# A four-layer conditioned residual block on one core: x1 as one fp32r product over 96 stacked rows, the class product over all 128 rows, and new stage orders before and after the loop

## The reference

```python
# layer 0: a low-rank product with weights of each entry's own (rank 30)
U = (mu @ W_dec + b_dec).reshape(B, 257, 30); param = einsum('bik,kj->bij', U, V)
x = x + (einsum('bsd,bde->bse', x, param[:, :-1]) + param[:, -1][:, None])
# layer 1: modulated linear layer
x = x + clip(einsum('blc,oc->blo', x * styles[:, None], weight) * dcoefs[:, None] + bias, -256, 256)
# layer 2: down to 64, relu, up to 256, both with weights scaled per entry
x = x + (relu(x @ w_down) @ w_up + x)
# layer 3: layer norms with gains picked by pathway, class and time ids, concatenated, MLP, layer norm
h = ln(ln(x, pw_g[pathway], pw_b[pathway]), cp_g[comp], cp_b[comp]); t = ln(x, tm_g[time], tm_b[time])
s = ln(x, ms_g[scale], ms_b[scale]);  m, n, r = x + mlp_ln(memory / noise / resource state)
x = x + ln(silu(cat([w0*h, w1*t, w2*m, w3*n, w4*r, w5*s]) @ W1 + b1) @ W2 + b2)
```

## Time and profile before

| | before |
|---|---|
| median of 3 runs | 523.67 us (523.2 to 524.6) |
| the profiled execution | 521.21 us, of which the span is 519.4 us |
| mean granted TensorE clock | 0.994 of full speed |
| busy: PE, PE weight loads | 486.3 us (94%), 354.2 us (68%) |
| busy: DVE, ACT, POOL | 405.8 us, 336.3 us, 391.0 us |
| DMA | 61.78 MB, mean 119 GB/s |

### The profile page before, as it was taken

One profiled execution on the slowest core, in us unless ns is written; L12 is line 12 of the kernel. 1 busy time (PEld: TensorE's weight loads), 2 busy tenths in 40 slices (PEclk: granted clock), 3 DMA queues, 4 the chain that ended last, 5 costly groups with the idle time before them and its releaser, 6 DMA issues.

```text
span 519.4 us, 9425 instructions
## 1 busy us (share of the span) xinstructions
PE 486.3 (94%) x3198; PEld 354.2 (68%) x3198; DVE 405.8 (78%) x696; ACT 336.3 (65%) x638; POOL 391.0 (75%) x367
## 2 busy tenths in 40 slices
...
GB/s 299 247 304 208 203 20 124 163 73 135 83 127 81 77 171 56 191 24 223 0 229 17 205 43 173 74 136 112 106 142 63 175 47 90 49 21 145 40 2 81
DMA packets 34989, 61.78 MB, mean 119 GB/s; under 512 B 5017, under 2 KB 17413, under 8 KB 34580
## 3 DMA queue, kind: packets, MB, share of 16 engines
...
q10 hardware_dynamic: 864, 0.61, 0.4%
...
## 4 chain that ended last, share of the span: by engine, by line
PE 79%; POOL 6%; DVE 5%; DMA 4%; issue 3%; ACT 2%; SPq 0%; DVEq 0%; POOLq 0%; ACTq 0%
PE ps_c L902 11%; PE ps_c L904 11%; PE ps_c L903 10%; PE ps_d L948 9%; PE ps_d L962 5%; PE ps_a L976 5%; PE ps_b L902 3%; PE ps_b L903 3%; PE ps_b L904 3%; PE ps_b L935 2%; PE ps_a L988 2%; DMA set_wdec<-in_nets_rows 2%; PE ps_a L994 2%; PE ps_b L994 2%; DMA set_wdec<-in_W_dec 1%
## 5 line engine op out<-in xcount | busy, mean ns | idle before, releaser
L1507 POOL DMA_INDIRECT pw_rows<-in_pw,gidx x64 | 65.0, 1016 | 17.9 <-issue 17.4
L948 PE MATMUL ps_d<-xm_t,l_w 128*128 128x512 f32 x128 | 59.0, 603 | 2.2 <-POOL xm_t L1516 2.2
L1209 ACT ACTIVATE h<-h,nb_h,rstd_h 128x256 f32<-128x256 f32 x64 | 33.3, 591 | 33.1 <-POOL nb_h L1531 33.0
L1240 ACT ACTIVATE tm_t_h<-ps_a 128x1024 fp32r<-128x1024 f32 x16 | 16.4, 1026 | 45.6 <-DVE ps_a L1413 45.6
L1516 POOL TENSOR_TENSOR xm_t<-x_t,style 128x1024 f32<-128x1024 f32 x16 | 30.5, 1905 | 20.2 <-DVE x_t L1345 20.1
L948 PEld LDWEIGHTS ps_d<-xm_t,l_w 128*128 128x128 f32 x128 | 23.1, 190 | 26.8 <-issue 24.2
L1546 POOL TENSOR_TENSOR h<-xhat,pw_rows 128x1024 f32<-128x1024 f32 x16 | 38.0, 2378 | 4.1 <-ACT xhat L1209 4.1
L1565 POOL TENSOR_TENSOR w_up<-up_rep,ugub 128x1024 f32<-128x1024 f32 x16 | 38.0, 2372 | 2.2 <-issue 2.0
L1551 POOL TENSOR_TENSOR h<-h,pw_rows 128x1024 f32<-128x1024 f32 x16 | 38.3, 2394 | 1.3
L1567 POOL TENSOR_TENSOR w_up<-w_up,ugub 128x1024 f32<-128x1024 f32 x16 | 38.1, 2382 | 1.3
L902 PE MATMUL ps_b<-w_h,act_t_l 128*128 128x256 f32 x128 | 37.7, 294 | 0.4 <-DVE act_t_l L1450 0.4
...
## 6 DMA issues: line engine op xcount, KB each, us to landing
...
pw_rows<-in_pw,gidx POOLq DMA_INDIRECT x64, 3.7
...
```

The lines of the kernel that those rows point to most:

```text
L948: m = eng.matmul(ps_l1[:, o, :], l1_w[:, k, o * P:(o + 1) * P], xm_t[:, k, :], start=k == 0, stop=k == KB - 1)
L1209: m = eng.activation(out[:, j, :], src[:, j, :], ACT.Identity, bias=nb[k][:, j:j + 1], scale=rstd[k][:, j:j + 1])
L1507: eng.indirect_dma_start(pw_rows[c.ring][:, j, :], None, t["pw"], bass.IndirectOffsetOnAxis(ap=gidx[c.ring][:, j:j + 1], axis=0)).then_inc ...
```

## The change

Six edits, the last one in all engines but SP:

1. V is loaded over 96 rows (three copies). `act_vhigh` makes its fp32r copy `v_st`, `v_vlow` replaces rows 64 to 95 by V's low half. `t_st` becomes 96 rows of fp32r.
2. `act_th1` copies t to a tile of its own (`t_f`, in the free rows of the index tile), `act_th2` writes three rounded copies of it instead of one, and a new stage `g_tlow` on POOL replaces the first by t's low half.
3. `pe_x1` makes, per half of the features, one fp32r matmul over the 96 rows.
4. `pe_cp` multiplies over all 128 rows where it took strips of 24, and `v_gains` leaves the second strip's class columns at zero.
5. `v_pads` clears all of `gain_tab` and `t_st` as well.
6. New `begin` and `end` tables on PE, ACT, DVE and POOL; in the loop's tables only `(g_tlow, 2)` is new.

```diff
         def pe_x1(eng, c):
...
-            wait(eng, a_th, c.n + 1)
+            if first(c):
+                eng.wait_ge(c_v, 2)
+            wait(eng, a_th, 2 * c.n + 2)
+            wait(eng, g_tl, c.n + 1)
             for k in range(KB):
-                rows = slice(k * RP, k * RP + RK)
-                m = eng.matmul(ps_x1[:, k, :], v_rep[rows, k * P:(k + 1) * P], t_st[rows, :], start=True, stop=True)
+                m = eng.matmul(ps_x1[:, k, :], v_st[:, k * P:(k + 1) * P], t_st[:, :], start=True, stop=True)
...
         def pe_cp(eng, c):
-            for j in (0, 2, 1, 3):
-                rows = slice(j // 2 * STRIP, j // 2 * STRIP + CLS)
-                m = eng.matmul(out[:, j, :], onehot[c.ring][rows, j * P:(j + 1) * P], gain_tab[rows, 0:D],
-                               start=True, stop=True)
+            for j in range(CT):
+                m = eng.matmul(out[:, j, :], onehot[c.ring][:, j * P:(j + 1) * P], gain_tab[:, 0:D], start=True, stop=True)
...
         def act_th1(eng, c):
-            wait(eng, p_x1, c.n)
-            out = t_st[0:RK, :].rearrange("r (q j s) -> r q j s", j=4, s=S)
+            wait(eng, g_tl, c.n)
+            out = t_f.rearrange("r (q j s) -> r q j s", j=4, s=S)
...
         def act_th2(eng, c):
-            wait(eng, a_th1, c.n + 1)
-            eng.activation(t_st[RP:RP + RK, :], t_st[0:RK, :], ACT.Copy).then_inc(a_th, 1)
+            wait(eng, a_th, 2 * c.n + 1)
+            wait(eng, p_x1, c.n)
+            for lo in (0, RP, 2 * RP):
+                m = eng.activation(t_st[lo:lo + RK, :], t_f, ACT.Copy)
+            m.then_inc(a_th, 1)
...
+        def act_vhigh(eng, c):
+            eng.wait_ge(d_wts, 48)
+            eng.activation(v_st[:, :], v_rep[:, :], ACT.Copy).then_inc(c_v, 1)
+        def v_vlow(eng, c):
+            eng.wait_ge(c_v, 1)
+            low = slice(2 * RP, 3 * RP)
+            eng.tensor_tensor(v_st[low, :], v_rep[low, :], v_st[low, :].bitcast(F32), ALU.subtract).then_inc(c_v, 1)
+        def g_tlow(eng, c):
+            wait(eng, a_th, 2 * c.n + 2)
+            low = t_st[0:RK, :]
+            eng.tensor_tensor(low, t_f, low.bitcast(F32), ALU.subtract).then_inc(g_tl, 1)
...
-                             (pe_dec, 11), (pe_style, 0), (pe_dec, 12), (pe_dec, 13), (pe_dec, 14), (pe_dec, 15),
+                             (pe_dec, 5), (pe_style, 0), (pe_dec, 6), (pe_dec, 7), (pe_dec, 8), (pe_dec, 9),
```

More of the change, by code:

```diff
@@ L188, in conditioned_residuals @@
         ugub = sb("ugub", [P, CT, 2 * D])
-        idx_ch = [sb(f"idx_ch{r}", [CLS, CH], I32) for r in range(2)]
+        idx_t = [sb(f"idx_t{r}", [2 * RP, CH]) for r in range(2)]
+        idx_ch = [tile[RP:RP + CLS, :].bitcast(I32) for tile in idx_t]
+        t_f = idx_t[0][0:RK, :]
         gidx = [sb(f"gidx{r}", [P, CT], I32) for r in range(2)]
```

224 lines of the change are left out of this document (116 added, 108 removed).

## The result

The changed kernel took **535.12 us** (median of 4, 533.41 to 535.51) against 523.43 (median of 4, 523.16 to 524.6): ratio 1.021, 95% interval 1.019 to 1.024. The forecast was 521.0. The profiled execution took 535.51 against 521.21, so 14.3 us are to be explained; the medians lie only 11.7 apart, since the profiled execution of the kernel before is 2.2 us faster than its median. Ratios leave out executions that were disturbed, two of e16's twelve among them (811.6 and 973.5 us), and the time given for e16 is the median of the other ten.

A forecast was written before the change was run, and what follows sets the result against it. PE was taken to bound the loop, and chains of waits the start and end. Loop -5.9, start +4.4 and end -1.2 gave -2.7: 521.0 us as a median, with a range of 517.0 to 525.0.

The forecast's parts named there:

- Loop, -5.9: x1 and the class product on PE in the loop: 0.45 us gained in each of 13 chunks, -5.9 us.
- the rival of 0.31: Loop, x1: 96 rows cost a change of strips, gain only 0.31 us a chunk, 522.9 us; chance 0.09.
- Covers on ACT and POOL, 0: In the loop: ACT's extra copies (+1.25 us) and POOL's low half (1.28 us) lie under existing waits, cost 0.
- (a): Before the loop: style, behind decode group 5, leaves PE idle 2.8 us for its data; decode ends at about 29.5.
- a rival of 0.14: Before the loop: PE's clock falls in two idle stretches, +3.8 us, 524.8 us in all; chance 0.14.
- The prediction's own sign of being wrong: In the changed profile: l1(0) before 42, a granted clock below 1.00 before 500, or slots still at 27.8 us.
- (b): Before the loop, more steps in chunk 0: l1(0) starts at 44.4, where it was 40.25, +4.15 us.
- (c): From l1(0) to l1(2), some time comes back: l1(2) starts at 86.3 against 83.76, +2.5 us.
- (d): POOL's steps between style(2) and style(3): style(3) at 112.2, where it was 108.29; 1.9 us more for the chunks behind.
- The end, -1.2: Behind the loop: the new order shortens waits of tm(14) and tm(15), -1.2 us, bounds -2.7 and +1.
- The bounds: Before the loop: the new orders cost +4.4 us, bounded at -1 (stage waits under others) and +7 (the clock).

The follow-up runs named there:

- e16: The edits with old begin and new end, ACT's copies of chunk 4 early, POOL's low half of chunk 2 right behind wup(1): 520.8 us, ratio 0.995.
- e4: Changed kernel with the style product back behind decode group 11 and its addition on ACT behind the last turn: 530.64 us, ratio 1.013.
- e5: Changed kernel with idle products put into PE's four long idle stretches before the loop: 535.46 us, ratio 1.022.
- e14: Arithmetic of the kernel before, run in the changed kernel's begin and end orders: 539.44 us, ratio 1.028.
- e1: All arithmetic edits, with begin and end in the orders of the kernel before and the new steps put in: 531.58 us, ratio 1.014.
- e2: Changed kernel with only its begin put back to the old order, the new end kept: 529.6 us, ratio 1.012.

## Why the prediction was wrong

- **Loop, -5.9:** right. 0.47 us a chunk for the 0.45 taken. The 96 rows are free (the rival of 0.31 is out), and x1 runs at fp32r's pace.
- **Covers on ACT and POOL, 0:** right for the loop.
- **(a) style, +2.8:** the wait was 3.03 us, as forecast; e4 shows 4.3 us. (Style moved ahead of six decode groups, 6 to 11; ten then stand behind it.) The missing 1.3 are the fall of the clock, 2.76 us for 1.50 (e5) in the twelve products behind style; it stood beside as a rival of 0.14. It was the rival's mechanism, and there were five falls instead of two. The prediction's own sign of being wrong, a granted clock below 1.00 before 500, thus came at 20 us.
- **(b) l1(0), +4.15:** +9.4. Of the 5.25 missing, 2.95 lie ahead of x1(0), which began at 42.95 and not at 40. (a)'s clock, 1.3, is in them. So is a term that the forecast's chain did not have, ScalarE's copies of t: they ended at 41.48, 1.1 us behind the gather of chunk 0 (40.41), because ScalarE began th1(0) some 2.6 us after t(0)'s last product. ACT's timeline in the changed kernel:

```profile
38.37 1.11 ACT L1185 ACTIVATE idx_t<-ps_b 30x128 f32<-30x128 f32 x4 [3.42 <-remote]
39.57 1.91 ACT L1196 ACTIVATE t_st<-idx_t 30x512 fp32r<-30x512 f32 x3
```

The other 2.3 are the second fall: at half clock l1(0) came 6.7 us behind x1(0) and not 4.4; in e5, at full clock, it was 4.2.
- **(c) l1(0) to l1(2), -1.6:** +7.4. **This is the step that failed.** The prediction took 3.9 us for the gains, from a place where POOL was gathering, and added a late DVE to an unchanged duration. Moved beside style(1) and wup(1) the same operations took 9.0 us (69.89 to 78.91), so l1(1) to l1(2) was 27.3 and not 21.5. And from l1(0) to l1(1) the 2.7 us that were to fall out of the chain did not (23.5 us for 20.4 forecast): w1's sum on DVE beside POOL took longer as well (twice 1.6 us for 0.7), and up(0) ran at half clock (3.75 for 2.02).
- **(d), +1.9:** +2.5, near.
- **The end, -1.2:** from l1(13) to the end -0.8, near only by luck: x1(14) and x1(15), which the -5.9 of the loop has already, are 0.9 of it, so the new end itself came to +0.1. The waits of 1.50 and 1.19 went; hht(14) and hht(15) wait 0.73 and 0.68 in their place (for DVE). e14 puts the new end at -0.2 without the edits. From e1 to e2 it is -1.4, but that only takes back what the edits' new steps cost at the old end (+0.5 where the two x1 alone give -0.9), a cost that the forecast had at nothing.
- **The bounds.** The price of the beginning was put at +4.4 and bounded at +7 by clock falls alone; it came to 19.2, and to 18.8 in e14, which has none of the edits. Of the 14.8 between 4.4 and 19.2, 5.25 belong to (a) and (b), 9.0 to (c) and 0.6 to (d). Each step was costed with durations of the old neighbourhood, and its own error fell on a chain without slack.

With the old beginning and the new stages placed better (e16) the same edits gave 0.5% less time than before, as much as the forecast had for the whole change.

**Open.** Why th1(0) starts late: the profile puts 3.42 us of ScalarE's idle time to "remote"; it is there in e14 too (3.40), so it comes with the order. Whether a beginning exists in which the whole 5 us of loop and end show: in e16's profiled execution l1(4) is still 8.2 us later than before. And what the clock cost behind l1(0), since the idle products of e5 stood in the way themselves.
